# Reordering one slot of a delta-rule attention stage: the first inverse product, the second state update and the second output product change places

## The reference, cut to what matters

```python
def step(S, inp):
    q_t, k_t, v_t, g_t, b_t = inp
    Sk = jnp.einsum('bhkv,bhk->bhv', S, k_t)
    delta = jnp.einsum('bhv,bhk->bhkv', v_t, k_t) - jnp.einsum('bhv,bhk->bhkv', Sk, k_t)
    S = jnp.exp(g_t)[..., None, None] * S + b_t[..., None, None] * delta
    o_t = jnp.einsum('bhkv,bhk->bhv', S, q_t)
    return (S, o_t)
```

## Time and profile before

| | before |
|---|---|
| median of 3 runs | 1834.06 us |
| profiled execution | 1840.0 us, span 1838.2 us |
| mean granted clock of TensorE | 0.948 of full speed |
| PE busy in the span | 1586.9 us (86%) |
| DVE busy | 1209.4 us (66%) |
| POOL busy | 957.5 us (52%) |
| ACT busy | 811.1 us (44%) |

### The profile page before, as it was taken

One profiled execution on the slowest core, in us unless ns is written; L12 is line 12 of the kernel. 1 busy time (PEld: TensorE's weight loads), 2 busy tenths in 40 slices (PEclk: granted clock), 3 DMA queues, 4 the chain that ended last, 5 costly groups with the idle time before them and its releaser, 6 DMA issues. The chain is left out here.

```text
span 1838.2 us, 75886 instructions
## 1 busy us (share of the span) xinstructions
PE 1586.9 (86%) x32268; PEld 1184.1 (64%) x32268; DVE 1209.4 (66%) x3029; ACT 811.1 (44%) x1898; POOL 957.5 (52%) x1197
## 2 busy tenths in 40 slices
PE   7579999999999999999999999659999994889950
PEld 6235666666666666666666666648888883878840
DVE  1478888888889889889888888315555552222214
ACT  1355565665565665566566556211111110333313
POOL 0145545545445545544554554205777775677853
PEclk9789999999999999999999999769999997999985
DMA  6345565665656665665665664434555541798557
GB/s 271 96 97 111 120 132 112 133 135 116 132 119 134 132 132 124 135 138 129 131 128 126 121 131 101 98 102 150 165 160 165 160 141 35 214 252 221 92 97 238
DMA packets 565041, 253.97 MB, mean 138 GB/s; under 512 B 458320, under 2 KB 532688, under 8 KB 563808
## 3 DMA queue, kind: packets, MB, share of 16 engines
q1 hardware_dynamic: 412640, 209.15, 44.2%
q10 hardware_dynamic: 133632, 20.98, 6.3%
q0 software_dynamic: 18432, 18.99, 5.9%
HBM read 177.68 MB, written 71.37 MB: 135 GB/s over the span
## 5 line engine op out<-in xcount | busy, mean ns | idle before, releaser
L376 PE MATMUL delta_p_j<-delta_xt,delta_w 128*128 128x512 f32 x768 | 387.3, 629 | 24.7 <-DMA delta_xt<-in_xt 18.6
L595 DVE SCALAR_TENSOR_TENSOR delta_kq<-delta_hist,cw,delta_kq 128x512 f32<-128x512 f32 x384 | 289.9, 755 | 30.2 <-ACT delta_kq L747 23.1
L912 POOL TENSOR_TENSOR delta_sd<-state,eg_end 128x256 f32<-128x256 f32 x128 | 129.5, 1012 | 247.5 <-DVE state L677 247.4
L1273 POOL DMA_INDIRECT slot_tokens<-mix_tokens,mix_slot x192 | 189.9, 989 | 65.4 <-issue 61.1
L740 ACT ACTIVATE delta_hist<-delta_p_j 128x512 f32<-128x512 f32 x192 | 114.1, 594 | 248.4 <-PE delta_p_j L376 224.0
L376 PEld LDWEIGHTS delta_p_j<-delta_xt,delta_w 128*128 128x128 f32 x768 | 133.3, 193 | 135.9 <-issue 121.1
L881 POOL TENSOR_SCALAR delta_n<-delta_n 128x8 f32<-128x8 f32 x64 | 15.4, 241 | 276.1 <-DVE delta_n L626 276.1
L796 ACT ACTIVATE delta_kpv<-delta_kpv,delta_root 128x64 f32<-128x64 f32 x512 | 135.5, 341 | 16.3 <-ACT delta_xit L782 16.3
L1367 PE MATMUL expert_p_h<-expert_xbt,w 128*88 128x128 f32 x1024 | 126.4, 277 | 13.2 <-ACT expert_xbt L1410 12.6
L1396 DVE SCALAR_TENSOR_TENSOR expert_gate<-expert_gate,expert_p_h 88x256 f32<-88x256 f32 x64 | 26.7, 417 | 168.4 <-ACT expert_gate L1416 112.6
L1367 PEld LDWEIGHTS expert_p_h<-expert_xbt,w 128*88 128x88 f32 x1024 | 115.9, 158 | 29.9 <-ACT expert_xbt L1410 27.2
(11 more groups left out here) (147 smaller groups left out, 3596.9 us busy)
## 6 DMA issues: line engine op xcount, KB each, us to landing
delta_xd<-x_scratch SPq DMA_DIRECT2D x256, 128.0 KB
delta_w<-in_wqkv SPq DMA_DIRECT2D x64, 416.0 KB
w<-in_w SPq DMA_DIRECT2D x64, 352.0 KB
delta_eg<-eg_rows SPq DMA_DIRECT2D x128, 130.0 KB
n_scratch<-delta_kkq ACTq DMA_DIRECT2D x128, 128.0 KB
mix_ot<-ot SPq DMA_DIRECT2D x16, 1024.0 KB
w<-in_w SPq DMA_DIRECT2D x64, 176.0 KB
delta_xd<-x_scratch SPq DMA_DIRECT2D x128, 64.0 KB
```

Source lines behind the costliest of these rows:

```text
L376: mm = pe.matmul(view(p_j, 512 if n == 2 else 0, (1, 512)), w[e][:, (ch * 3 + n) * 128:(ch * 3 + n) * 128 + 128], xt[m // 8 % 2][:, ch * 5 ...
L595: ve.scalar_tensor_tensor(out, view(hist[e], i * 2 * 518 + tap, (259, 2), (1, 256)), cw[:, column:column + 1], out, ALU.mult, ALU.add).the ...
L912: po.tensor_tensor(view(sd, 0, (128, 2), (C, 2), (1, C)), view(state, first_pair(group) * 128, (C, 2), (128, 2), (1, C)), view(s.eg_end, g ...
L1273: po.indirect_dma_start(out=s.tok.ap(), out_offset=bass.IndirectOffsetOnAxis(ap=slot[i % 2][:, k:k + 1], axis=0), in_=tokens[:, i:i + 1], ...
```

## The change

Four calls move, on three engines, in the part of the slot that works on `two_`. TensorE calls `inverse_r` ahead of `chain_state`, and the third projection ahead of `chain_update`; VectorE calls `conv_values` ahead of `update`; ScalarE calls `output` behind `history(m, 2)`, and so behind the turning of the inverse and the second half of `scale_values`. GpSimd and SP keep their order. Nothing is computed otherwise.

```diff
@@ TensorE
+                if is_macro(mi):
+                    inverse_r(mi)
                 if two_:
                     chain_state(*two_)
-                if is_macro(mi):
-                    inverse_r(mi)
                 if is_macro(m):
                     project(m, 1, proj_v)
...
                     inverse_rx(mi)
+                if is_macro(m):
+                    project(m, 2, proj_q)
                 if two_:
                     chain_update(*two_)
-                if is_macro(m):
-                    project(m, 2, proj_q)
@@ VectorE
                     horner(mi, rx_done, 16, y1_out)
+                if is_macro(m):
+                    conv_values(m)
                 if two_:
                     update(*two_)
-                if is_macro(m):
-                    conv_values(m)
@@ ScalarE
                     last_tap(m, 2, yv[m % 2][:, :], tap_v)
-                if two_:
-                    output(*two_)
                 if t % 2 == 0 and 0 <= (t - 4) // 2 < NG:
                     turn_inverse((t - 4) // 2)
                     store_turned((t - 4) // 2)
...
                     history(m, 2, proj_q)
+                if two_:
+                    output(*two_)
+                if is_macro(m):
                     last_tap(m, 1, kq[m % 2][:, 512:1024], tap_q)
```

## The result

| | before | after |
|---|---|---|
| median | 1839.24 us (14 runs, 1826.78 to 1847.03) | 1856.52 us (14 runs, 1848.05 to 1865.6) |
| profiled execution, span | 1840.0, 1838.2 us | 1859.88, 1858.1 us |
| ratio, 95% interval | | 1.0098, 1.0076 to 1.0120 |

The changed kernel is 1.0% slower. The median before is that of all its runs beside the changed kernel, the three known at the prediction among them. 1851 us was predicted for a median before of 1834.06, so 1.0092; measured is 1.0098. The sum came out right, but several of its terms did not: the even slots cost less than predicted, the odd slots more, and that the total met is in part luck.

What follows compares the result with a forecast made beforehand. A loop over TensorE and VectorE, through y2, was taken as the bound; 11.5 + 15.7 - 5.6 - 5 + 1 gave +17.6, taken as +17 us: 1851 against a median of 1834.06, 8-in-10 range 1822 to 1867.

Steps and rivals of the forecast that it cites:

- The output copy in even slots: ScalarE's output copy ends later, so VectorE's update and y2 wait: +0.41 us per even slot, 11.5 us.
- GpSimd's lock: GpSimd's line 900 holds up VectorE's query convolution, line 595, before even slots: about +0.56 us each, 15.7 us.
- The mask: VectorE's mask (line 638) no longer waits for line 425's products: 0.2 us sooner in each of 28 slots, -5.6 us.
- The stalls absorbed: Part of TensorE's own stalls vanishes in its longer wait for y2 in even slots: -5 us, nothing to 8 possible.
- The odd slots: Inverse product delays VectorE's residual, about +0.5 us, offset by removed waits: between -0.3 and +0.3, taken as 0.
- The worst case: Odd slots lose +0.5 us too (14 us), nothing absorbed, inverse product's data waits delay the chain: 1865 to 1875 us, chance 0.12.
- The third projection: On TensorE it fills the wait for u: 14 us where TensorE bounds, nothing where line 472 waits for y2.
- The tail: Last slots without projections, bound by the chain, with output copy and inverse product in the way: +1 us, -1 to +4.
- faster: Rival: the update does not delay y2 and TensorE's wait for u is gone: 1812 to 1820 us, chance 0.18.
- the lock doesn't bite: Rival: VectorE's convolution wins the port or another GpSimd instruction lies there: +3 us, 1837 us, chance 0.22.
- (3): Sign: TensorE's waits of line 472 for line 659 grow to 0.5 us and more in nearly every slot.
- (4): Sign: GpSimd's line 912 waits longer for the state; line 595's first instruction takes 1.2 to 1.3 us, before 0.75.

Runs made afterwards that it cites:

- e4: The changed kernel with GpSimd's state decay moved behind the scaling of the keys; 1856.13 us, ratio 1.0067 to the kernel before.
- e3: The changed kernel with TensorE's first inverse product back behind the second state product; 1848.56 us, ratio 1.0024 to the kernel before.
- e2: The kernel before with the moves on VectorE and ScalarE alone, TensorE's order unchanged; 1854.37 us, ratio 1.0078.
- e6: The changed kernel with y2 ahead of the state update on VectorE; 1861.71 us, ratio 1.0089 to the kernel before.
- e7: The changed kernel with inverse product back behind state product, y2 ahead of update, GpSimd's decay behind key scaling; 1826.31 us, ratio 0.9926 to before; again 0.9949.

## Why the prediction was right, and where it was not

- **What bounds the kernel**: right. y2's place on VectorE decided, and in 57 of 57 slots line 472 started at its end. TensorE's wait for u vanished and bought nothing directly.
- **The output copy in even slots**: right. Predicted were y1 to y2 3.47 us for 3.06; it is 3.47 in the slot shown and 3.42 in the median of the even slots, +0.36 for +0.41. In the means it goes from 3.14 to 3.44: 8.4 us for 11.5.
- **GpSimd's lock**: the mechanism was right, the size a little high: +0.42 us on line 595 for +0.56, 11.8 us for 15.7. The prediction's working has a slip: by its rows line 900 ends at U + 3.09, not 3.05, so the meeting was to last 3.09 - 2.47 = 0.62 us. It did: line 901 ended 0.62 us after line 595's start, but only 0.42 of it reached the sum. The mask and the residual, with an operand in PSUM, keep their 1.22 and 0.41 us beside GpSimd. The Trainium skill (SBUF — State Buffer, section "Who interferes with whom") gives the rule that the first of the two keeps the port for its whole instruction. The trace agrees for lines 901 and 595, where line 595 gives way. It does not agree for GpSimd's power (line 906, 128 x 8), which in the kernel before runs from 710.13 to 711.79 beside line 595 and leaves it its 2.32 us. Taking the lock away (e4) gave back 7.6 us in the trace and 0.3% in the medians, less than 11.8: in the odd slots nothing changed (17.58 and 17.57).
- **The mask**: it starts 0.26 us sooner behind y2 (0.59, now 0.33 in the mean of the even slots): 7.3 us for 5.6.
- **The stalls absorbed**: taken as 5 us. The three terms above give 8.4 + 11.8 - 7.3 = 12.9 in the means, and the even slots grew by 12.3, so as a term of its own it is 0.6 us. Part of it is inside the terms: by the medians the output copy costs 10 us, by the means 8.4. That stalls vanish in the wait for y2 can be seen: 26 of the 28 even slots take 17.41 to 17.48 us, where before they lay between 16.6 and 20.
- **The odd slots**: this is the step that failed. "1.0 - 0.44 leaves about +0.5 us" for the inverse product and an offset, "I take 0 for the slot"; measured is +0.37 us, 10.4 us in all. The two halves can be read apart in the means of the odd slots, counted from line 472. The residual comes 1.07 us later (8.02, now 9.09), as predicted; the wait for the blocks falls from 0.44 to 0.07, and the first substitution comes 0.66 later (10.31, now 10.97), for the predicted 0.5. What was to offset it fell short: y1 to y2 takes 0.23 us less (3.10, now 2.87) and y2 to line 472 0.06, together 0.29 for the 0.5 taken. The mask's part of the offset could not come: in all 28 odd slots VectorE waits for the residual, 1.81 us in the mean (0.76 before), and what it wins ahead of that wait is lost in it. The range, -0.3 to +0.3, did not hold the sum. Against e3 the inverse product's move costs still more, 17.58 - 16.82 = 0.76 us, since there the first substitution waits only 0.25 us for the blocks, so less of the delay is absorbed; why the blocks come earlier in e3 was not followed up. By the medians of the runs that move costs 0.74%, 14 us. The worst case (0.12) had said "the odd slots lose their +0.5 as well", and its first part is nearly what happened.
- **The third projection** was priced only by u's wait, "nothing where line 472 then waits for y2". That is right for the wait. Not seen was that the output copy's new place behind the history needs it: without it VectorE's and ScalarE's moves cost 10 us more, in the odd slots (e2 against e3).
- **The tail**: +1.2 for +1.

So the total was right with even slots 4 us under their terms (12.3 for 16.6) and odd slots 10 over, and a lucky -3.4 behind the stage: the terms up to the last state update come to 23.4 us in the profiled executions, for the predicted 17.6, and the medians of all runs differ by 17.3. That these agree within 1 us is luck. Of the rivals "faster" fell with the output copy's end, which came 0.4 us behind the convolution's; "the lock doesn't bite" by line 595's 2.74 us. All five signs named in the prediction are seen, (3) in 54 of 57 slots, and (4) with the first instruction of line 595 at 1.16 us, just under the 1.2 to 1.3 named.

What stays open is what stops TensorE in most odd slots some 7 to 9 us behind line 472, and why the blocks come at different times from kernel to kernel.

## What to carry to other kernels

A move within one engine's order has two prices: what now comes later, and what the engine's own stops now fall into; in the kernel before a stop behind the chain's product left the residual where it was in 9 slots, and the same stop ahead of it delays it. Where an instruction that sets the end stands behind another on the same engine, swapping the two helps only by what does not come back elsewhere: here y2 ahead of the update alone showed no gain (e6), since the mask and GpSimd's work are timed by the update, and it paid in a kernel where GpSimd's order and the inverse product's place were changed as well (e7). A change of several moves should be taken apart before it is judged: three of these four belonged together and cost nearly nothing (1.0024), the fourth cost 0.55% alone and 0.74% on top of the others.

## What the runs showed of the hardware

Line 595, a VectorE instruction with both inputs in SBUF, takes longer when it meets line 901, a GpSimd instruction on SBUF, and the price grows with the overlap: three instructions of line 595 took 2.32, 2.51, 2.74 and 3.07 us as line 901 ended before, 0.38, 0.62 and 0.95 us after their start, so about 0.2 us less than the overlap each time. It goes the other way too: in e4 GpSimd's line 877 (128 x 384) starts while VectorE's convolution of the values runs and takes 1.44 us, where it takes 1.01 beside the mask. And where line 595 had been held up, GpSimd's next instruction took longer in turn: line 907 has a mean of 2087 ns in the changed kernel and 1676 in e4, where line 595 was not held up (1675 before, there line 906). GpSimd's power (128 x 8, 1.7 us) lay beside line 595 before too, from 710.13 in the slot of the earlier trace rows, and line 595 kept its 2.32 us. That this GpSimd instruction, long but with small operands, does not hold VectorE is known here of this one alone, and its cause was not looked for.
